# Float32 products of the routed expert blocks replaced by split products, with the splits on three engines

## The reference, cut to what matters

```
def _moe(x_flat, Wr, Wg, Wu, Wd):            # x_flat 1024 x 256, 8 experts, two per row
    logits = x_flat @ Wr.T
    top_logits, top_idx = jax.lax.top_k(logits, TOP_K)
    probs = jax.nn.softmax(top_logits, axis=-1)
    cw = jnp.zeros((T, NUM_EXPERTS), x_flat.dtype)
    cw = cw.at[jnp.arange(T)[:, None], top_idx].add(probs)
    hg = jnp.einsum('eih,th->eti', Wg, x_flat)         # 512 x 256 per expert
    hu = jnp.einsum('eih,th->eti', Wu, x_flat)
    y = jnp.einsum('ehi,eti->eth', Wd, jax.nn.silu(hg) * hu)   # 256 x 512 per expert
    return jnp.einsum('eth,te->th', y, cw)
```

## Time and profile before

| what | value |
|---|---|
| median of 3 runs | 769.14 us (768.36 to 769.21) |
| the profiled execution's own time | 771.2 us |
| its span, first to last instruction | 769.4 us |
| PE busy | 603.2 us (78%), 3606 matmuls |
| DVE busy | 478.2 us (62%) |
| ACT busy | 276.4 us (36%) |
| POOL busy | 263.1 us (34%) |
| mean granted TensorE clock | 0.892 of full |
| chain that ended last: line 745 of PE (products) | 19% of the span |

### The profile page before, as it was taken

The page is one execution under the profiler, slowest core; times in us unless marked ns, Lnnn a source line. Parts: engine busy times, 40 slices in busy tenths (PEclk is TensorE's granted clock), DMA queues, the critical chain, the costliest instruction groups (busy, mean ns, idle before and its releaser), DMA issues.

```text
span 769.4 us, 10430 instructions
## 1 busy us (share of the span) xinstructions
PE 603.2 (78%) x3606; PEld 402.4 (52%) x3606; DVE 478.2 (62%) x1048; ACT 276.4 (36%) x535; POOL 263.1 (34%) x242
## 2 busy tenths in 40 slices
PE   3933667877576869999549998888878799999990
PEld 2721445655452658888215555455445556666660
DVE  6869997969767865594577877867764211221223
ACT  1376433323101222354206664554535332222220
POOL 3157557645275643456661001001025001111111
PEclk9975769989867999999558999999989999999996
DMA  5101200000011300259996664260003958888835
GB/s 184 53 27 55 78 2 0 1 1 0 0 45 36 83 0 1 77 104 167 205 234 83 84 83 58 31 84 1 3 22 119 331 216 289 306 293 280 302 143 177
DMA packets 45779, 81.93 MB, mean 106 GB/s; under 512 B 7424, under 2 KB 37312, under 8 KB 42784
## 3 DMA queue, kind: packets, MB, share of 16 engines
q1 hardware_dynamic: 43856, 76.15, 38.5%
q0 software_dynamic: 1872, 5.13, 1.7%
HBM read 65.56 MB, written 15.51 MB: 105 GB/s over the span
## 4 chain that ended last, share of the span: by engine, by line
PE 38%; DVE 10%; DMA 3%; issue 2%; ACT 2%; POOL 1%; SPq 0%; POOLq 0%; DVEq 0%; ACTq 0%
PE bank L745 19%; DVE small L1671 5%; PE bank L992 4%; PE bank L969 4%; PE bank L942 4%; PE bank L739 4%; DMA pieces<-P 2%; PE bank L944 1%; PE bank L971 1%; POOL P L2071 1%; DVE mtok L1682 1%; PE bank L1009 1%; DMA yt<-results 1%; ACT PTa L1257 1%; DVE XA L1700 0%
## 5 line engine op out<-in xcount | busy, mean ns | idle before, releaser
L1671 DVE TENSOR_REDUCE small<-bank 128x1 f32<-128x256 f32 (+3 forms) x256 | 107.5, 482 | 14.1 <-PE bank L944 13.2
L745 PE MATMUL bank<-wb,xt 128*128 128x512 f32 x184 | 82.8, 592 | 0.0
L1976 POOL TENSOR_TENSOR al<-hm,ah 128x512 fp32r<-128x512 f32 (+1 forms) x28 | 40.9, 1462 | 92.0 <-ACT ah L1220 92.0
L942 PE MATMUL bank<-Ks,Qs 96*128 96x256 bf16 (+3 forms) x256 | 67.5, 331 | 5.3 <-DVE small L1671 3.7
L1915 DVE TENSOR_TENSOR bhm<-bsg,bank 128x512 f32<-128x512 f32 x23 | 15.8, 688 | 83.8 <-PE bank L745 83.8
L969 PE MATMUL bank<-Qs,Ks 99*128 99x512 bf16 (+3 forms) x256 | 59.5, 309 | 7.2 <-issue 6.8
L944 PE MATMUL bank<-maskb,identb 128*128 128x128 bf16 x256 | 55.8, 236 | 0.0
L1542 DVE TENSOR_TENSOR_SCAN S<-AT,U 128x512 f32<-128x512 f32 x32 | 49.7, 1553 | 8.2 <-POOL QS L1994 7.9
L1257 ACT ACTIVATE PTa<-bank 128x512 f32<-128x512 f32 (+1 forms) x96 | 43.7, 528 | 30.4 <-PE bank L971 30.1
L1257 ACT ACTIVATE PTb<-bank 128x512 f32<-128x512 f32 (+1 forms) x96 | 43.7, 529 | 28.4 <-PE bank L971 28.0
L969 PEld LDWEIGHTS bank<-Qs,Ks 99*128 99x128 bf16 x256 | 25.5, 100 | 49.3 <-issue 32.4
(11 more groups left out here) (332 smaller groups left out, 1517.0 us busy)
## 6 DMA issues: line engine op xcount, KB each, us to landing
wb<-e_pack SPq DMA_DIRECT2D x23, 1536.0 KB, 7.0
pieces<-P SPq DMA_DIRECT2D x12, 512.0 KB, 10.0
Qs<-pieces SPq DMA_DIRECT2D x48, 128.0 KB, 5.4
Ks<-pieces SPq DMA_DIRECT2D x48, 128.0 KB, 6.1
stg<-w_pack SPq DMA_DIRECT2D x18, 256.0 KB, 2.7
wf<-t_pack SPq DMA_DIRECT2D x12, 256.0 KB, 2.7
sorted_rows<-blank SPq DMA_DIRECT2D x1, 2944.0 KB, 13.5
yt<-results SPq DMA_DIRECT2D x8, 256.0 KB, 5.0
```

What stands on the lines that cost most here:

```text
L745: last = nc.tensor.matmul(outap, a, b_, start=start and i == 0, stop=stop and i == n - 1, **kw)
L942: nc.tensor.matmul(banks[b][:, o:o + w], Q[0:96, h, i * P:(i + 1) * P], K[0:96, h, 0:w], start=True, stop=False)
L1671: last = nc.vector.tensor_reduce(mxv[:, i, h:h + 1], banks[b][:, o:o + w], AX.X, ALU.max, negate=True)
L1976: nc.gpsimd.tensor_tensor(al[0:M, s % 3, :], hm[0:M, s % 3, :], ah[0:M, s % 3, :].bitcast(F32), ALU.subtract).then_inc(*alr.tick(s))
```

## The change

Inside the blocks, every product becomes three split products. The rows (`xh`, `xl`) and the inner rows (`hT`, `hTl`) are split by ACT (high: the copy out of PSUM that was there, now with a float32r output) and DVE (low: PSUM minus high). The weights are split for each block after their load: ACT casts gate, up and down to `wh` and `wdh` (three casts of 1024 elements for each partition), DVE subtracts for gate and up (`wl`), POOL for down (`wdl`). A new entry `bw` in ORDER places them, for block i + 1, around the work of block i. The split weights lie in two buffers each, in SBUF that was `wb2`'s and that of `XTh`/`XTl`; `wb2`, `xga` and `owner_i` move, and the first 8 blocks now take their rows from `rows`, the next 11 from `xga`.

In the diff, the last three pieces (`elif op == "bw"`) stand in the loops of ACT, DVE and POOL.

```diff
-XG_PARTS = [(0, XGA), (XGA, XGA + NC * CH // P), (XGA + NC * CH // P, BLOCKS)]
+XG_PARTS = [(0, NC * CH // P), (NC * CH // P, NC * CH // P + XGA), (NC * CH // P + XGA, BLOCKS)]
...
-        m, _ = plan([("wb2", [EW], F32)], slot_at[1])
+        m, o = plan([("wb2", [EW], F32)], x1_at + 10240)
...
+        m, _ = plan([("wh", [2, 2, KC, EI], F32R), ("wl", [2, 2, KC, EI], F32R)], slot_at[1])
+        moe.update(m)
+        m, o = plan([("wdh", [2, 4, D], F32R), ("wdl", [2, 4, D], F32R)], xt_at)
...
-        ORDER.append(("bx", 0))
+        ORDER += [("bx", 0), ("bw", 0, 0), ("bw", 0, 1), ("bw", 0, 2)]
         for i in range(BLOCKS):
             if i + 1 < BLOCKS:
-                ORDER.append(("bx", i + 1))
+                ORDER += [("bx", i + 1), ("bw", i + 1, 0)]
             ORDER.append(("gu", i))
+            if i + 1 < BLOCKS:
+                ORDER.append(("bw", i + 1, 1))
             if i >= 1:
                 ORDER.append(("dn", i - 1))
             ORDER.append(("ht", i))
+            if i + 1 < BLOCKS:
+                ORDER.append(("bw", i + 1, 2))
...
             for i in range(2):
                 block_weights(i)
-            sp.wait_ge(*w_split.upto(len(JOBS) - 1))
             for j in range(2):
                 sp.wait_ge(s_put[j], 16 * NT)
             sorted_part(0)
-            sorted_part(1)
             for i in range(2, NWB):
                 block_weights(i)
             sp.wait_ge(*mm.upto(("wout", 3, 1)))
+            sorted_part(1)
             sorted_part(2)
...
             def block_in(i):
-                xt = moe["xt"][:, i % 2]
-                pe.wait_ge(*bxh.upto(i))
-                pe.wait_ge(s_wb[i % NWB], 16 * (i // NWB + 1))
+                xh, xl = moe["xh"][:, i % 2], moe["xl"][:, i % 2]
+                pe.wait_ge(*bxl.upto(i))
                 for half, who in ((0, bgate), (1, bhid)):
                     b = 2 * half + i % 2
                     claim(b, who, i)
-                    w = raw_half(i, half)
-                    product(banks[b][:], [(xt[:, k], w[:, k]) for k in range(KC)]).then_inc(*mm.tick(("gu", i, half)))
+                    pe.wait_ge(*wsl.upto((i, half)))
+                    wh, wl = moe["wh"][:, i % 2, half], moe["wl"][:, i % 2, half]
+                    terms = []
+                    for k in range(KC):
+                        terms += [(xh[:, k], wh[:, k]), (xl[:, k], wh[:, k]), (xh[:, k], wl[:, k])]
+                    product(banks[b][:], terms).then_inc(*mm.tick(("gu", i, half)))
...
             def block_out(i):
-                pe.wait_ge(*bht.upto(i))
+                pe.wait_ge(*htl.upto(i))
+                pe.wait_ge(*wdl_ready.upto(i))
...
+                for m in range(EI // P):
+                    h_, l_ = moe["hT"][:, i % 2, m * P:(m + 1) * P], moe["hTl"][:, i % 2, m * P:(m + 1) * P]
+                    terms += [(h_, wh[:, m]), (l_, wh[:, m]), (h_, wl[:, m])]
...
+                elif op == "bw":
+                    _, i, half = it
+                    act.wait_ge(s_wb[i % NWB], 16 * (i // NWB + 1))
...
+                    elif i >= 2:
+                        act.wait_ge(*mm.upto(("dn", i - 2) if half == 2 else ("gu", i - 2, half)))
+                    if half == 2:
+                        ins = nc.scalar.copy(moe["wdh"][:, i % 2], raw_down(i))
+                    else:
+                        ins = nc.scalar.copy(moe["wh"][:, i % 2, half], raw_half(i, half))
...
+                elif op == "bw" and it[2] < 2:
+                    nc.vector.tensor_tensor(moe["wl"][:, i % 2, half], raw_half(i, half), moe["wh"][:, i % 2, half].bitcast(F32),
+                                            ALU.subtract).then_inc(*wsl.tick((i, half)))
...
+                elif op == "bw" and it[2] == 2:
+                    nc.gpsimd.tensor_tensor(moe["wdl"][:, i % 2], raw_down(i), moe["wdh"][:, i % 2].bitcast(F32), ALU.subtract)\
+                        .then_inc(*wdl_ready.tick(i))
```

More of the change, by code:

```diff
@@ L149, in build @@
         XA = sb("XA", [NT, D], F32)
+        xt_at = cursor[0]
         XTh = sb("XTh", [KC, NC * CH], F32R)
@@ L234, in block_rows_of @@
         def block_rows_of(i):
-            if i < XGA:
-                return moe["xga"][:, i, :]
+            if i < NT:
+                return rows[:, i, :]
             if i < XGA + NT:
-                return rows[:, i - XGA, :]
+                return moe["xga"][:, i - NT, :]
             return moe["xgc"][:, i - XGA - NT, :]
@@ L243, in build @@
         moe.update(m)
-        m, o = plan([("bsg", [2, EI], F32), ("bhm", [2, EI], F32), ("hT", [2, EI], F32), ("xt", [2, KC, P], F32)], mlp_at)
+        m, o = plan([("bsg", [2, EI], F32), ("bhm", [2, EI], F32), ("hT", [2, EI], F32R), ("hTl", [2, EI], F32R), ("xh", [2, KC, P], F32R),
+                      ("xl", [2, KC, P], F32R)], mlp_at)
         assert o <= mlp_at + 20480
@@ L343, in build @@
         share_set = tally("row_shares_set")
-        bxh = tally("block_rows_turned")
+        wsh = tally("block_weights_high")
+        wsl = tally("block_weights_low")
+        bxh = tally("block_rows_high")
+        bxl = tally("block_rows_low")
+        htl = tally("block_hidden_low")
+        wdl_ready = tally("block_down_low")
         bgate = tally("block_gate")
@@ L695, in sorted_part @@
                 src = sorted_rows[b0 * P:b1 * P, :].rearrange("(b p) d -> p b d", p=P)
-                dst = (moe["xga"][:], rows[:], moe["xgc"][:])[j]
+                dst = (rows[:], moe["xga"][:], moe["xgc"][:])[j]
                 sp.dma_start(dst, src).then_inc(s_xg[j], 16)
@@ L1357, in _ @@
                         act.wait_ge(*mm.upto(("gu", i - 2, 1)))
-                    nc.scalar.copy(moe["xt"][:, i % 2], banks[6][:, 0:D].rearrange("p (k n) -> p k n", k=KC)).then_inc(*bxh.tick(i))
+                    nc.scalar.copy(moe["xh"][:, i % 2], banks[6][:, 0:D].rearrange("p (k n) -> p k n", k=KC)).then_inc(*bxh.tick(i))
+                elif op == "bw":
+                    _, i, half = it
+                    act.wait_ge(s_wb[i % NWB], 16 * (i // NWB + 1))
+                    if i == 0:
+                        act.wait_ge(*mm.upto(("st", N_HEADS - 1, 2)))
+                        if half == 2:
+                            for pr in range(2):
+                                act.wait_ge(*mm.upto(("wout", 3, pr)))
+                    elif i >= 2:
+                        act.wait_ge(*mm.upto(("dn", i - 2) if half == 2 else ("gu", i - 2, half)))
+                    if half == 2:
+                        ins = nc.scalar.copy(moe["wdh"][:, i % 2], raw_down(i))
+                    else:
+                        ins = nc.scalar.copy(moe["wh"][:, i % 2, half], raw_half(i, half))
+                    ins.then_inc(*wsh.tick((i, half)))
                 elif op == "gu":
@@ L1916, in _ @@
                         .then_inc(*bhid.tick(i))
+                elif op == "bx":
+                    i = it[1]
+                    dve.wait_ge(*bxh.upto(i))
+                    if i >= 2:
+                        dve.wait_ge(*mm.upto(("gu", i - 2, 1)))
+                    nc.vector.tensor_tensor(moe["xl"][:, i % 2], banks[6][:, 0:D].rearrange("p (k n) -> p k n", k=KC),
+                                            moe["xh"][:, i % 2].bitcast(F32), ALU.subtract).then_inc(*bxl.tick(i))
+                elif op == "bw" and it[2] < 2:
+                    _, i, half = it
+                    dve.wait_ge(*wsh.upto((i, half)))
+                    dve.wait_ge(s_wb[i % NWB], 16 * (i // NWB + 1))
+                    nc.vector.tensor_tensor(moe["wl"][:, i % 2, half], raw_half(i, half), moe["wh"][:, i % 2, half].bitcast(F32),
+                                            ALU.subtract).then_inc(*wsl.tick((i, half)))
+                elif op == "ht":
+                    i = it[1]
+                    dve.wait_ge(*bht.upto(i))
+                    if i >= 2:
+                        dve.wait_ge(*mm.upto(("dn", i - 2)))
+                    nc.vector.tensor_tensor(moe["hTl"][:, i % 2, :], banks[4][:], moe["hT"][:, i % 2, :].bitcast(F32),
+                                            ALU.subtract).then_inc(*htl.tick(i))
                 elif op == "dn":
```

27 lines of the change are left out of this document (18 added, 9 removed).

## The result

The changed kernel takes 804.34 us (median of 4 runs, 804.04 to 806.19), the kernel before 769.17 on the same chip (4 runs, 768.36 to 769.50): a ratio of 1.0464, 95% interval 1.0446 to 1.0482, so 35 us slower. The forecast was 803, in a range of 780 to 818. The profiled execution took 804.61 us, its span is 802.8; before it was 771.2 and 769.4.

The account below looks back on a forecast made before the run. TensorE bound the kernel before at 5.81 us a block; in-order queues and the DVE/POOL port lock would make it 7.35. 22 x (7.35 - 5.81) = 34 us on 769.1 gives 803, range 780 to 818.

Parts of the forecast that it names:

- TensorE's part: Expert blocks: split products and transposes need 4.9 us a block, 0.9 less than now; 20 us gained if TensorE set the pace.
- Work of the others: Each block: ACT gets 4.8 us of work, DVE 4.75, POOL 4.1; every engine alone would stay under 5 us.
- The port: SBUF port shared by DVE and POOL: `wl`, `wl` and `wdl` exclude each other, 4.83 us of turns in each block.
- The two loops without the port: Queues with a free port: 6.1 us a block through weight loads over two blocks, 5.6 or 5.4 through casts over one.
- Order A: `wdl` before gate-weight `wl`: one-block loop through `ys`, result DMA, `wdl`, `wl`, `bhm`, `wl`, taking 7.6 us a block.
- order B: Gate-weight `wl` before `wdl`: up-weight `wl` waits for `wdl`, a two-block loop of 14.1 us, 7.05 us a block.
- Start and end: Ends of the kernel: first cast and subtraction cost 2.3 us, the last step is shorter by about that; net taken as 0.
- The sum: Whole kernel: 22 x (7.35 - 5.81) = 34 us slower, ends counted 0; median from 769.1 to 803 us.
- Rival 1: Expert blocks: the lock bites little, `wdl` falling beside PSUM reads and `xl`; 6.1 us a block, 775 us; chance 0.13.
- Rival 2: Expert blocks: queues absorb the loops, TensorE's 4.9 us sets the pace; 749 us, halfway 759; chance 0.06.
- Rival 3: Expert blocks: TensorE's clock falls to half for a third of the time, 0.5 to 1 us a block; 814 to 825; chance 0.11.
- The page's rule: POOL's result DMA: if it waits while DVE holds the port, it falls behind gate-weight `wl`, order B is certain, near 798 us.

Follow-up runs that it names:

- the second order: Changed kernel with gate-weight subtraction a block earlier still, other splits before the down products, load buffers freed by their last reader: 757.37 us, ratio 0.9859 to the kernel before.
- none: Changed kernel without POOL's subtraction for the down weights, third down product reading the high part again: ratio 1.0138 to the kernel before; repeated on another chip, 1.0173.
- memsets: Changed kernel with POOL's down-weight subtraction replaced by two memsets of the same tile: ratio 1.0174 to the kernel before.
- subtraction on VectorE: Changed kernel with the down-weight subtraction moved from POOL to VectorE: 779.08 us, ratio 1.0108 to the kernel before.
- the other order without the early free: Changed kernel with the next block's three splits issued before the down products, row transposes last, buffer release unchanged: ratio 1.0221 to the kernel before.
- the fast version: Changed kernel with the next block's three splits before the down products and weight buffers reloaded once split: 759.61 us, ratio 0.9882; repeated, 757.38 us, 0.9849.
- the run with POOL's queue turned round: Changed kernel with POOL's down-weight subtraction for the next block put ahead of the previous block's result DMA: ratio 1.024 to the kernel before.

## Why the prediction was right

It was right in its time and in its cause, though two terms of its sum were off, by 1.5 and by 2 us in opposite directions, and it was luck that they cancelled. Its steps:

- **TensorE's part**, 4.9 us a block: right, 4.86 to 4.89 in most steps of the second order, where TensorE is full; 5.02 to 5.04 in the first. The gain of 0.9 exists and was never on the path of the changed kernel.
- **Work of the others.** Right within 0.05 an operation: casts 1.05 for 1.06, `hTl` 0.67 for 0.69, `xl` 0.42 for 0.43, `wdl` 2.39 for 2.37, result DMA 0.78 + 1.00 for 0.79 + 0.97.
- **The port**, 4.83 us of turns a block: right in kind. Without POOL's reads `wl` takes 1.22, with them up to 3.30. The stretch has the size given, up to 2.1 where up to 2.3 was put: 3.28 = 2.19 that `wdl` still had to go + 1.09. The 1.09 is the 1.1 that the prediction itself read from the earlier trace rows.
- **The two loops without the port**, 6.1 and 5.4: right, 6.06 to 6.16 in three runs (none, memsets, subtraction on VectorE) and 5.31. The term that stands for landing was taken at 7.0; the other order without the early free, with 6.3 to 12.0 and a median of 8.4, shows that it is no constant.
- **Order A or order B.** The prediction could not tell them apart by 0.1 us and took the middle. It was order A: `wdl` came first by 0.20. Its count was good: from the end of `bhm` (702.99) it is 3.35 to the next `wdl` and 3.54 to the next `wl`, where it had 3.4 and 3.5. For A it had 7.6, and 7.42 was measured; the size that was off is `wl`, counted at 1.23 from the end of `wdl` to `bhm` and costing 1.01, although its own gave 1.1. So 7.35 came out nearly right for half a wrong reason: the middle lay 0.25 below A as I had it, and A itself was 0.18 too long.
- **Start and end.** The start costs 1.4 where 2.3 was put. The last step was to be shorter by about those 2.3; it is 4.21, 3.2 below the steady 7.43, and before it was 0.2 below. The first step and the tail give back 0.3 each. Net -2.1 instead of 0.
- **The sum**: +34 for +33.4 in the spans. In the prediction's terms it is 22 x (7.43 - 5.82) = 35.5 for the steady step, where 34 was put, and -2.1 for the ends, where 0 was put. The time of order B was added up wrong: 22 x (7.05 - 5.81) is 27, which makes 796 and not 798.

**The rivals.** Rival 1, the lock bites little: wrong for the change as made (`wl` at 2.04), but its 6.1 is what the kernels get in which the lock has gone (6.06 to 6.16). Rival 2, faster at TensorE's pace: wrong, since its condition (`ys` 0.6 earlier) was not given; with another order and an earlier free its mechanism holds, at 757 instead of 749. Of the 8 us between, 22 x (5.12 - 4.9) makes 5 and 5.775 instead of 5.81 for the block before 1. The other 2 lie between medians and profiled executions: the latter are 771.2 and 757.1, 14 apart, the medians 12. Rival 3, the clock falls: half of it happened. The granted clock in the windows above is 0.91 to 1.00, and between 670 and 690 it was 0.87, so some stretches ran at 1.2 instead of 2.4 GHz; in one of them (675 to 677) products start 0.43 apart instead of 0.23. But the steady step stays 7.42 to 7.46 throughout, because the loop holds no instruction of TensorE: there `wl` only starts later behind `wdl`. In the fast version's windows above it was 1.00.

**The page's rule.** In the prediction the Trainium skill, SBUF — State Buffer, section SBUF: two separate sides, was weighed for a DMA that POOL issues: if it had to wait for `wl`, order B and 798 us would follow. The changed kernel could not show it, because the DMA always started before `wl` did (697.89 against 699.12). The run with POOL's queue turned round does: there the DMA starts inside a `wl` 19 times, with 0.92 of it to go, and takes 1.80 each time instead of 1.00, so it is held up by 0.80; the second order shows 1.80 to 1.94 in seven more. Where it began 0.26 before a `wl`, as at 681.74 above, it took 1.00. So such a DMA is held up here by a plain float32 subtraction. The page says it of a two-port mode, and further down, under Who interferes with whom, that a `tensor_tensor` was not seen to stall a DMA; with these 26 of 26 the runs say otherwise, and they decide. What in the DMA's issue has to wait was not isolated. It did not decide this change because the DMA came first, by 1.2 us. The section on the two sides has the lock only against a GpSimd operation that reads SBUF; the memset run agrees, with 1.23 beside 0.95.

What was not tried: `wdl` held back until `wl` is done in the changed order (order B by force), so that its 7.05 stays an estimate.

## What to carry to other kernels

Splitting work over engines pays only if the new pieces don't meet in a shared port and don't close a loop through an in-order queue: here TensorE's own work fell by 0.9 us a block, and the block grew by 1.6 because of a loop that never touches TensorE. List every loop (queue, buffer, port) with its period, since the longest hides the others and freeing one alone may show nothing: 0 us a block under the first loop, 0.75 to 1.17 once it is open. Put an operation that takes the shared port beside those that read PSUM, and free a load's buffer by its last reader rather than by the end of the block.

## What the runs showed of the hardware

- A float32 subtraction of 128 x 1024 with both inputs in SBUF takes 1.22 us on VectorE alone or beside POOL's memset (0.95), and up to 3.30 to 3.44 when it starts just behind POOL's subtraction of the same size (2.39). POOL's takes 2.39 to 2.43 in the changed kernel's blocks, where it starts first, and 2.59 to 3.13 when it starts inside one of VectorE (the other order with the early free, and the first block).
- An indirect DMA that POOL issues takes 1.00, and 1.79 to 1.94 when it starts inside such an operation of VectorE (26 of 26), ending about 0.88 after it. I had not expected to see it with plain float32.
- A load of 1536 KB lands in 6.3 to 12.0 us within one kernel (the other order without the earlier free); that bunched issues do it was argued, not isolated. At 0.92 of the DMA engines' time and 340 GB/s the median was 8.5 to 8.8 us with TensorE never waiting, so with loads issued early enough the landing time did not matter there.
